# Silu after a convolution: one ScalarE pass with a Silu table, where there were three passes and a VectorE product

## What is computed

```
h = layernorm(x) @ w_in[:, :48] + b_in          # folded into the convolution's weights
y = conv3x3(h, conv_w) + conv_b                 # 48 -> 24 channels, zero border
x = x + silu(y)                                 # silu(y) = y / (1 + exp(-y))
t = x + mixer(layernorm(x))                     # the next block starts with a norm
```

## Time and profile before

| What | Value |
|---|---|
| time, median of 3 runs | 3357.95 us (3356.18 to 3360.39) |
| the profiled execution's own time | 3362.17 us |
| its span, first to last instruction | 3360.4 us |
| PE busy | 2929.0 us, 87% of the span |
| VectorE busy | 1694.8 us, 50% |
| ScalarE busy | 1642.3 us, 49% |
| GpSimd busy | 366.1 us, 11% |
| chain that ended last, by engine | PE 67%, ACT 14%, DVE 7%, issue 6%, POOL 3%, DMA 2% |
| mean granted TensorE clock | 0.968 of full speed |

### The profile page before, as it was taken

How to read it: one execution, slowest core, us unless ns; L and a number is a source line. 1 busy time by engine, 2 the same in 40 slices (tenths; PEclk the granted TensorE clock), 3 DMA queues, 4 the chain that set the end, 5 groups by cost and what they waited for, 6 DMA issues and landing times.

```text
span 3360.4 us, 110185 instructions
## 1 busy us (share of the span) xinstructions
PE 2929.0 (87%) x49196; PEld 1851.3 (55%) x49196; DVE 1694.8 (50%) x2741; ACT 1642.3 (49%) x2947; POOL 366.1 (11%) x574
## 2 busy tenths in 40 slices
PE   6868889888898898988988889888898888988888
PEld 3537546466455573564744647447465474554754
DVE  5524556355553546544464544635457354573454
ACT  3642456633565435644266353663535635456245
POOL 4520010000100011001010011000110001100001
PEclk8989999999999999999999999999999999999999
DMA  2321000210001100110002100021000210001100
GB/s 79 66 64 48 2 16 5 52 33 2 16 19 44 27 2 17 35 47 7 2 18 53 33 1 2 18 53 34 2 2 19 53 33 1 2 19 33 33 1 16
DMA packets 28434, 84.79 MB, mean 25 GB/s; under 512 B 22002, under 2 KB 23138, under 8 KB 24114
## 3 DMA queue, kind: packets, MB, share of 16 engines
q1 hardware_dynamic: 26690, 72.55, 9.0%
q0 software_dynamic: 1280, 5.21, 0.6%
HBM read 61.70 MB, written 14.84 MB: 23 GB/s over the span
## 4 chain that ended last, share of the span: by engine, by line
PE 67%; ACT 14%; DVE 7%; issue 6%; POOL 3%; DMA 2%; SPq 0%; ACTq 0%; POOLq 0%; DVEq 0%
PE ps L1143 67%; ACT area_ty L858 2%; ACT lv L720 2%; ACT rs L725 2%; DMA f_all<-piece 2%; POOL piece L594 1%; ACT sq L708 1%; DVE xs L1113 1%; DVE area_hz L988 1%; POOL piece L598 1%; ACT area_hz L763 1%; ACT area_ty L810 1%; ACT area_ty L850 1%; ACT area_ty L816 1%; ACT sq L706 1%
## 5 line engine op out<-in xcount | busy, mean ns | idle before, releaser
L1143 PE MATMUL ps<-area_hz 32*49 32x147 f32 (+3 forms) x7180 | 363.6, 289 | 83.4 <-DVE area_hz L988 24.5
L1143 PE MATMUL ps<-area_ty,area_hz 113*64 113x49 f32 (+2 forms) x10240 | 411.5, 257 | 8.3 <-ACT area_ty L742 7.9
L834 ACT ACTIVATE area_hz<-ps 121x384 f32<-121x384 f32 (+2 forms) x256 | 129.6, 519 | 582.9 <-PE ps L1143 582.9
L1143 PE MATMUL ps<-sq,keep_sb 64*64 64x392 f32 (+1 forms) x1728 | 343.9, 541 | 71.2 <-ACT sq L708 44.4
L1143 PEld LDWEIGHTS ps<-area_hz 32*49 32x49 f32 (+3 forms) x7180 | 289.9, 151 | 176.8 <-issue 153.9
L1143 PEld LDWEIGHTS ps<-area_ty,area_hz 113*64 113x64 f32 (+2 forms) x10240 | 320.4, 133 | 81.6 <-issue 80.5
L1143 PE MATMUL ps<-area_ty,g_sb 56*112 56x192 f32 (+1 forms) x3712 | 311.6, 321 | 26.0 <-DVE area_ty L1085 19.7
L1143 PEld LDWEIGHTS ps<-area_ty,g_sb 56*112 56x112 f32 x3712 | 293.1, 173 | 44.7 <-issue 43.9
L1143 PE MATMUL ps<-xs,keep_sb 64*64 64x448 f32 (+1 forms) x1184 | 222.0, 549 | 87.5 <-DVE xs L1113 47.1
L1085 DVE COPY area_ty<-ps 120x896 f32<-120x896 f32 (+1 forms) x192 | 164.8, 858 | 237.0 <-PE ps L1143 237.0
L720 ACT ACTIVATE lv<-ps 128x448 f32<-128x448 f32 (+1 forms) x304 | 158.6, 522 | 222.8 <-PE ps L1143 222.8
(11 more groups left out here) (127 smaller groups left out, 4402.4 us busy)
## 6 DMA issues: line engine op xcount, KB each, us to landing
area_hz<-f_all SPq DMA_DIRECT2D x16, 2541.0 KB
xw<-x_in SPq DMA_DIRECT2D x8, 1568.0 KB, 6.8
y_out<-xs SPq DMA_DIRECT2D x32, 252.0 KB
f_all<-piece POOLq DMA_DIRECT2D x16, 317.6 KB, 4.5
area_hz<-raw_in SPq DMA_DIRECT2D x1, 2894.0 KB, 9.6
g_sb<-g_in SPq DMA_DIRECT2D x6, 355.2 KB
area_ty<-area_hz SPq DMA_DIRECT2D x128, 9.2 KB
g_sb<-g_in SPq DMA_DIRECT2D x2, 710.5 KB
```

The source lines that it names most:

```text
L834: act.activation(dst, src, ACT.Relu if st in (ST_H, ST_F2) else ACT.Copy).then_inc(sc_kept, 1)
L1143: return pe.matmul(o, a, b, start=start, stop=stop)
```

## The change

- ScalarE computes silu in one pass: `ACT.Silu` with the convolution's bias, two instructions of 128 x 784 a group from PSUM to `yc`; they signal `silued` themselves. The exponential, the logarithm, the second exponential, and VectorE's product are gone.
- Silu needs a table of its own. It is put in place before group 0's wait for `conved`, and the logarithm and exponential table is put back after the squares of pieces 0 and 1 of the norm that follows, ahead of its first logarithm.
- On PE the three idle products between center_mix(0) and center_mix(1) are gone, and move(1) stands ahead of variance_pair(0) instead of behind it.
- In the setup, two one-column instructions of VectorE that made biases (L913, L914) are gone.

```diff
-        N_WIN, N_SETUP_VE = 33, 34
+        N_WIN, N_SETUP_VE = 31, 32
...
+                act.preload_act_table_set("silu_and_others")
                 for g in range(GROUPS):
-                    k = (q * GROUPS + g) * 2
                     act.wait_ge(conved, q * GROUPS + g + 1)
                     for p in range(2):
                         act.activation(yc[g][:, 2 * p:2 * p + 2, :],
-                                       ps[:, 4 * g + 2 * p:4 * g + 2 * p + 2, 0:CW[g]], ACT.Exp, scale=-1.0,
-                                       bias=act_bias[:, 0:1]).then_inc(neg_exped, 1)
-                    for p in range(2):
-                        o = yc[g][:, 2 * p:2 * p + 2, :]
-                        act.wait_ge(neg_exped, k + p + 1)
-                        act.activation(o, o, ACT.Ln, bias=act_bias[:, 1:2]).then_inc(log1ped, 1)
-                    for p in range(2):
-                        o = yc[g][:, 2 * p:2 * p + 2, :]
-                        act.wait_ge(log1ped, k + p + 1)
-                        act.activation(o, o, ACT.Exp, scale=-1.0).then_inc(sigmoided, 1)
+                                       ps[:, 4 * g + 2 * p:4 * g + 2 * p + 2, 0:CW[g]], ACT.Silu,
+                                       bias=K("cb")).then_inc(silued, 1)
                 square(q, LN_MIX(0), 0)
                 for i in range(NP):
                     if i + 1 < NP:
                         square(q, LN_MIX(0), i + 1)
+                    if i == 0:
+                        act.preload_act_table_set("natural_log_exp_and_others")
                     invert(q, LN_MIX(0), i)
...
-            su(ve.tensor_scalar(act_bias[:, 0:1], K("cb"), -1.0, None, ALU.mult))
-            su(ve.tensor_scalar(act_bias[:, 1:2], K("cb"), 0.0, 1.0, ALU.mult, ALU.add))
...
                 for g in range(GROUPS):
-                    for p in range(2):
-                        k = (q * GROUPS + g) * 2 + p
-                        o = yc[g][:, 2 * p:2 * p + 2, :]
-                        ve.wait_ge(sigmoided, k + 1)
-                        ve.scalar_tensor_tensor(o, ps[:, 4 * g + 2 * p:4 * g + 2 * p + 2, 0:CW[g]], K("cb"), o,
-                                                ALU.add, ALU.mult).then_inc(silued, 1)
                     for c in range(CHUNKS):
...
                 center_mix(0)
-                keep_busy(2, 3)
                 center_mix(1)
+                move(1)
                 variance_pair(LN_MIX(0), 0)
-                move(1)
                 variance_pair(LN_MIX(0), 1)
```

More of the change, by code:

```diff
@@ L285, in build_kernel @@
         xs = sb("xs", [128, NTOK])
-        act_bias = sb("act_bias", [128, 2])
         sq = sb("sq", [128, 2, PT])
@@ L411, in build_kernel @@
             sem("mlp_up"), sem("gelu_done"), sem("mlp_down"), sem("mlp_added"), sem("tile_reordered"))
-        border, conved, neg_exped, log1ped, sigmoided, silued, conv_moved, conv_added = (
-            sem("border_zeroed"), sem("conv_made"), sem("conv_negative_exp"), sem("conv_log"),
-            sem("conv_sigmoid"), sem("silu_done"), sem("silu_at_its_image"), sem("conv_added"))
+        border, conved, silued, conv_moved, conv_added = (
+            sem("border_zeroed"), sem("conv_made"), sem("silu_done"), sem("silu_at_its_image"),
+            sem("conv_added"))
         terms_loaded, table_made, table_stored = (
```

## The result

The changed kernel takes 3323.88 us (median of 4 runs, 3323.03 to 3324.64), against 3357.06 us (3355.40 to 3360.39, 4 runs) for the kernel before on the same chip: a ratio of 0.989 with a 95% interval of 0.9875 to 0.9904, 33.2 us less. A second timing, in a later group of runs, gave 3326.27 us and 0.9897 (0.9881 to 0.9913). The forecast was 3330 us. One run of a later kernel (the kernel before with the earlier table) took 4076.66 us; it is a slow execution, and counts in no figure here.

A forecast was written before the change was run, and what follows sets the result against it. ScalarE's chain was taken to bound the convolution's tail. Savings of 8.1 + 26.2 + 0.4 = 34.7 us, less 7 for TensorE's clock, gave 28 us and 3330 us against a 3357.95 us median; range 3317 to 3343, the forecast's own 3324 to 3336.

The forecast's parts named there:

- What bounds: Convolution's tail: ScalarE sets the pace; what counts is when it is free of silu and done with the fourth Exp.
- Group 0: Between the groups: short silu ends PE's wait before move(0), 8.1 us over eight quads; PE then bound by its taps.
- Group 1: Tail from group 1's first Silu: fourth Exp over at 12.7 instead of 15.97, 3.27 us a quad, 26.2 us in all.
- The load of the Silu table costs nothing: Before group 0's silu: the 1.28 us load fits in ScalarE's 3.5 us wait for the last taps.
- The rule against the change: Skill page: each table switch costs about 2.66 us, 1.38 of it drain; by it the sum would be 11 us smaller.
- The drain: Rival, chance 0.06: each load on the path costs 1.38 us more, 11 us in all, giving 3341 us.
- TensorE's clock: Sparser PE tail lets the clock fall to 1.2 GHz: 1.1 us in six quads, 7 us lost.
- the lower level behind 9.4: PE's clock at 1.2 GHz from 9.4 us after group 1's first Silu, expected in about six of eight quads.
- the rival in which the clock stays up: Rival, chance 0.20: no lower clock in the tail, so 34.7 us come off, 3323 us.
- two places of the kernel before: Sparse PE stretches followed by 1.2 GHz: the first in all quads but one, the second in 4 of 8.
- if the gain of a quad is found and lost again outside the tail: Sign of a wrong prediction: a quad's gain in the convolution's tail disappears elsewhere in the kernel.
- the change in the setup: Head of the kernel: two small instructions gone, 0.15 us each and a wait each, some 0.4 us by estimate.

The follow-up runs named there:

- the kernel before with the earlier table: Kernel before, two of four inverse-table loads moved behind the first quad's forward-table load on SP's queue: 3356.62 us, ratio 0.9986.
- the order alone: Kernel before with PE's new order (three idle products gone, move(1) ahead of the first variance), silu still in three passes and a product: 3366.0 us, ratio 1.0018.
- silu alone: Changed kernel with PE's old order put back (three idle products between the centrings, move(1) behind the first variance): 3337.16 us, ratio 0.9932.
- the experiment with one more load: Changed kernel with an extra Gelu table load directly ahead of the load between second square and first logarithm: 3346.26 us, ratio 0.9959.
- the earlier table: Changed kernel, two of four inverse-table loads moved behind the first quad's forward-table load on SP's queue: 3322.45 us, ratio 0.9882.
- the load under cover: Changed kernel with an extra Gelu table load ahead of the Silu table load, where ScalarE waits for group 0's last tap: 3324.38 us, ratio 0.9905.
- the program with both edits: Changed kernel with inverse-table loads moved behind the forward table, plus one idle product in each PE tail gap: 3311.47 us (0.9863), again 3316.79 us (0.9878).

## Why the prediction was right, and where it was off

**What bounds.** Right: ScalarE's chain was the bound of the tail, and the time until ScalarE is free of silu is what counted. VectorE's product and ScalarE's passes fell off one for one only as far as they stood in that chain.

**Group 0.** Right in mechanism; that the size agrees (8.1 us forecast, 8.4 measured) is partly luck. PE no longer waits before the move, and the silu is over long before the taps. But what is left is not simply the old stretch less PE's wait of 1.00 us. In the changed kernel's second profile the shortest stretch from group 0 to group 1 is 8.60 us, 1.46 less than 10.06, while others take up to 10.06 (first profile) and 10.80 us (second), all at a granted clock of 1.00. A standstill of PE in the taps explains only some of that: 0.28 and 0.34 us in two quads of the first profile, 1.58 us in the quad with 10.80, and none in the one with 10.06. The cause stays open. In the nine other profiles of kernels with Silu the eight stretches sum to 72.5 to 76.8 us, so that the saving is anything from 5.7 to 10.0 us. The load of the Silu table costs nothing, and not even a second one costs anything that shows.

**Group 1.** Right in size and in its steps. Silu takes 911 ns, 910 were taken. The first Ln was put at 4.5 us behind the first Silu and is at 4.46, the fourth Exp was to be over at 12.7 and is at 12.64, the mixer was to start at 14.4 and starts at 14.31. The load takes what it was said to, 1.28 us on ScalarE. It ends 0.8 us behind the variance that it overlaps in six of the eight quads, 0.7 in the fifth and 0.5 in the second; 0.9 were forecast. That nothing is gained by taking the three idle products out while they lie beside the passes fits the order alone, which lost. It does not show that they were worth nothing there, since without them and with the new place of the move the clock fell in every tail. The run with silu alone shows what I had put in no sentence: left in, they would have cost 1.8 us a quad, 14 us of the tails' 25.

**The rule against the change.** The drain is in none of the loads of these traces behind which ScalarE had work waiting, neither on the path nor under cover. That rival is out. But its price came out of the experiment with one more load nevertheless, half of it by TensorE, which shows that a time alone would have misled here.

**TensorE's clock.** This is the term that was mis-sized: "I expect the lower level behind 9.4 in about six of the eight", 7 us. The mechanism is there, at the place given, and mostly a little below the price given. The third quad:

```profile
1049.29 1.18 PE L1128 MATMUL ps<-sq,keep_sb 64*64 64x392 f32 x8 [1.48 <-ACT sq L705]
1050.40 4.63 PE L1128 MATMUL ps<-keep_sb 128*128 128x448 f32 x8
1054.96 1.21 PE L1128 MATMUL ps<-mix,area_ty 64*64 64x96 f32 x24
```

```profile
1043.00:1049.00 6.00, 3.52 (x40) 1.02 (x32) 3.67 (x6) 5.79 (x8) 0.00 (x0) 1.00 0.00 0
1049.00:1053.00 4.00, 3.71 (x12) 1.58 (x13) 3.03 (x3) 3.38 (x5) 0.00 (x0) 0.60 0.00 0
```

The idle products run to 1054.96, 15.03 us behind the first Silu (15.2 was said), 0.7 us later than with the clock up. But it happens in two quads of eight in this profile, one in the second (there with 1.9 us), four and two in two more kernels whose tail is the same (the earlier table, the load under cover): 9 of 32 tails, not 24. Seven of the nine cost 0.6 to 0.7 us, one 1.1 and one 1.9, where 1.1 was taken. By the tails' lengths over 14.3 that is 1.4 to 2.6 us a kernel instead of 7, and the time came out at the rival in which the clock stays up, 3323 us. The range that went with the forecast, 3324 to 3336 us, was drawn too narrow for its own terms: 0.8 us in five quads and 1.7 in all eight give 3327 to 3337, and with the spread of 4 us 3323 to 3341. The measured 3323.88 us lies just below the one and just within the other, and well within the whole range of 3317 to 3343. I had counted from two places of the kernel before, of which one falls nearly always and one in half of the quads, and had taken the tail for worse than the second; which it was not. The run with one more load shows that it does not take much more: with 2.36 to 2.58 us in place of 1.09 to 1.29, eight of eight fall. The nine tails all lie in the second, third, fifth and seventh quad, none in the sixteen tails of the other four; the third and the fifth fall in three profiles of four each. What sets these quads apart was not tried.

**What was missed.** "The load costs nothing" and "eight quads" took each quad to be alike. The first is not: its transform waits 6.87 us for a table whose load SP issues at 213 us whatever PE does. The mixer starts 10.6 us earlier than before (234.54, 245.09), the forward transform only 3.2 us (255.35, 258.58): 7.3 us are lost, more than that quad's gain from the change. The prediction named it as a sign of being wrong "if the gain of a quad is found and lost again outside the tail", and that holds for this quad. That it did not show in the sum is luck, with a reason outside the change: in this profile the first quad's silu starts 5.9 us earlier than in the profile before (211.5, 217.4), of which the change in the setup explains 0.4 by the forecast. The rest shows in PE's wait for GpSimd ahead of the first quad's norm, 17.80 us in this profile and 25.28 in the one before. That wait differs as much with nothing changed: 21.8 us in the changed kernel's second profile, and 20.4 and 12.5 us in the two profiles of the program with both edits.

## What to carry to other kernels

Cut a chain on the engine that sets the pace and look at once for what lay beside it: filler that was free under six passes cost 1.8 us a quad under two. Put a table load where its engine waits anyway. On the path it costs its own 1.28 us less what it overlaps, and more only through what the idle time does to another engine. And before a few microseconds of such an edit are believed, look at the granted clock of the whole profile: one program differed by 16 us between two executions with equal tails.

## What the runs showed of the hardware that was not expected

- No drain shows around a table load in these traces: it takes 1.28 us each time, starts 0.02 us or less behind the instruction before it, the next one starts 0.01 to 0.02 us behind it where it has nothing to wait for, and two in a row take 2.57 us (624.08 to 626.65).
- The clock's low stretches between 270 and 3300 us last 3.4 or 6.8 us at 1.2 GHz, but for two of 10.2 us. In the tail, with PE waits of 0.9 to 1.3 us and 1.5 to 1.8 us around one variance of 0.89 us, one came in 9 of 32 cases; with waits of 2.4 to 2.6 us and 1.5 to 1.8 us in eight of eight; with one idle product in each gap in none of 24.
- In nine of the thirteen profiles PE stands still once in the first quad for 2.8 to 5.1 us without a wait that the trace names, in the mixer's first stage or in the taps. In the changed kernel the share of the DMA engines in the stretch around it is high (0.73 between 243 and 249 us), but the other four profiles have no such stop. What PE lacks there was not tried.
- How long one issue holds SP changed with what had been issued before it: the load of the forward table held it for 20.85 us right behind the four loads of the inverse table, and for 0.33 us, at 193.23 us, where only two of them stood ahead (the changed kernel with the table earlier).
